# GpSimd's batch loop written out, each batch's row scatter issued behind the next batch's group power

## The chip, the cores and the metric

The kernel runs on one core of one Trainium2 chip. The metric is the device time of one execution in microseconds (us), lower is better. The engines are TensorE (PE; its weight loads are PEld), VectorE (DVE), ScalarE (ACT), GpSimd (POOL) and SyncE (SP, which here only issues DMAs).

## The reference

A transformer block with modulated norms over x of 4 batches, 512 tokens and 256 features. Cut to what matters:

```python
mod = (silu(c) @ wmod).reshape(4, 6, 1, 256)           # sa, ca, ga, sb, cb, gb
h = layernorm(x) * (1 + ca) + sa
# retention with 16 heads of 16 features, decay gamma per head, causal
scores = einsum('bhnd,bhmd->bhnm', q, k) * gamma ** (n - m)
ret = einsum('bhnm,bhmv->bhnv', scores, v)
norm = (ret - mean) * rsqrt(var + 1e-5)                # mean, var per batch and head, over tokens and features
x = x + ga * ((silu(h @ wg + bg) * (norm * gn_w + gn_b)) @ wo + bo)
h = layernorm(x) * (1 + cb) + sb
# 8 experts of 256 -> 512 -> 256, each token goes to its 2 best
logits = h @ gate;  weights = softmax(top2(logits))
x = x + gb * sum over the two experts of weight * (silu(h @ w0) * (h @ w1)) @ wo_e
```

## The kernel before

Retention part. The four batches are done one after another, each in chunks of 128 tokens (4 a batch). For a chunk TensorE makes the scores of four groups of four heads (L1330), VectorE multiplies them by the decay (L912), TensorE multiplies them with the values (L1342) into two PSUM banks `ret`. When chunk 3 of batch b is through, VectorE takes statistics of `ret` (`group_norm`, L917 to L941: L923 and L925, an averaging matmul on TensorE, L935), and the power -1/2 of the variances is GpSimd's: `group_power(b)` waits for L935 and does a tensor_tensor with pow on 128x2 numbers (L452, by the helper of L437). VectorE turns the result into scale and shift (L938 to L941), ScalarE applies them (`group_normed`, L635), VectorE multiplies by the gate (L946), TensorE projects out (`out_rows`, L1366), VectorE adds to x (L957), and SP stores x (L362, 512 KB a batch).

Second norm and routing. VectorE takes row statistics (L781 to L791); `modulate(b)` on GpSimd makes the power of the row variances (L457, by L437), VectorE normalizes the rows into `h2` (`second_norm`, L963 to L968, which waits for that power and for `h2_free`), and GpSimd scales and shifts `h2` (L460, L463). TensorE turns `h2` (L1378) and makes the logits; VectorE picks the two best experts and computes the rows of a DRAM buffer, `routed`, into which each token goes (`idx`, L1030). GpSimd then scatters: `scatter(b)` issues eight indirect DMAs of 128 rows of 266 numbers (L488), and `scatter_done(b)` waits until all have landed and adds to `h2_free`. There is one `h2`, so the next batch's `second_norm` can't write before that.

Order of the work. It is written out by hand for each engine, in program order, with semaphores between the engines. The batches are overlapped: while batch b finishes (group norm, projection out, second norm, routing), the projections and chunks 0 to 2 of batch b+1 are done. GpSimd also makes, for every chunk, a copy of q spread over heads, `qx` (`expand_q`, L447, 128x1024, needed by TensorE for that chunk's scores; ScalarE makes the other half at L628), the scaled output weights (`scale_wo`, L470) and the bias in x (`add_bias`, L477, L480). Its queue in a round of the loop (L512 to L522) is: group power of b; `expand_q(b+1, 0)`; `modulate(b)`; `expand_q(b+1, 1)`; `scale_wo(b+1)`; `expand_q(b+1, 2)`; `add_bias(b+1)`; `expand_q(b+1, 3)`; `scatter(b)`; `scatter_done(b)`. The loop turns three times, for b of 0, 1, 2; the group power of batch 3 stands behind the loop (L553). ScalarE, VectorE and TensorE have loops of three rounds of their own; theirs begin at chunk 3 of a batch and end behind chunk 2 of the next.

Expert part. The rows in `routed` are worked off in 39 tiles of 128 rows, each of one expert. The first 9 tiles (EARLY) are rows of the first batches and are begun while batch 3 finishes: SP loads a tile's rows (L372), `out_rows(3)`, its second norm and its routing are placed between the steps of these tiles. A tile takes TensorE, ScalarE and VectorE work, a gather of gate rows by GpSimd (`fetch_gb`, L527), and an accumulating indirect DMA into the output (`add_rows`, L545). `added_ok` is a count that VectorE waits for before it reuses a buffer of `meta` or `ey`; GpSimd starts it with 4 (L552). The scatter of batch 3 is issued in pairs between the `add_rows` of tiles 2 to 5 (L565).

Of the kernel before, what the change touches and what calls it, by code (L numbers as in the profile page):

```python
# [30 lines left out]
B, S, D = 4, 512, 256  # L31
# [64 lines left out]
def adaln_block(nc, x, wq, bq, wk, bk, wv, bv, wg, bg, wo, bo, gn_w, gn_b, gamma,  # L96
                gate_k, w0, w1, wo_e, c, wmod, out):
    ctx = ExitStack()
    with ctx:  # L99
# [124 lines left out]
        def sems(names):  # L224
            return [sem(n) for n in names.split()]
# [24 lines left out]
        added, added_ok, pool_passed, dve_passed, act_passed = sems("added added_ok pool_passed dve_passed act_passed")  # L250
# [55 lines left out]
        def wait(eng, pair):  # L306
            eng.wait_ge(pair[0], pair[1])

        def settle(eng, pairs, passed):


            for s, v in pairs:
                eng.wait_ge(s, v)
            eng.sem_inc(passed, 1)
# [4 lines left out]
        def grp(b, n):  # L319

            return b * (4 * NC) + n
# [83 lines left out]
        def _(pool):  # L405
# [29 lines left out]
            def power(out_, in_, n, done):  # L435

                g.tensor_tensor(out_, in_, mhalf[:, 0:n], ALU.pow).then_inc(done, 1)  # L437

            def expand_q(b, c):


                if c == 0:
                    wait(pool, front.drains(b, "q0"))
                pool.wait_ge(scored, grp(b, 4 + 4 * (c - 1) + 2))
                q = qT[:, 0, c * P:(c + 1) * P].unsqueeze(1).broadcast_to([P, HPT, P])
                m = hmask[:, :].unsqueeze(2).broadcast_to([P, HPT, P])
                g.tensor_tensor(qx[:, 0, :].rearrange("p (h n) -> p h n", h=HPT), q, m, ALU.mult).then_inc(qx_pool, 1)  # L447

            def group_power(b):

                wait(pool, tail.drains(b, "gn"))
                power(grs[:, :], gve[:, :], FT, grstd)  # L452

            def modulate(b):

                pool.wait_ge(var2, b + 1)
                power(rs2[:, :], ve2[:, :], NC, rstd2)  # L457
                hv = h2[:, :, 0:D]
                pool.wait_ge(h2n_ready, NC * b + NC)
                g.tensor_tensor(hv, hv, gsc[:, bass.ds(b, 1), 2 * D:3 * D].broadcast_to([P, NC, D]),  # L460
                                ALU.mult).then_inc(h2m_ready, 1)
                pool.wait_ge(h2m_ready, b + 1)
                g.tensor_tensor(hv, hv, gsc[:, bass.ds(b, 1), D:2 * D].broadcast_to([P, NC, D]),  # L463
                                ALU.add).then_inc(h2_ready, 1)

            def scale_wo(b):

                if not (isinstance(b, int) and b == 0):
                    settle(pool, [(tail.full, tail.filled(b - 1, "wo23"))], pool_passed)
                g.tensor_tensor(wob[:, :, :], wo_s[:, :, :], gsc[:, bass.ds(b, 1), 0:D].broadcast_to([P, FT, D]),  # L470
                                ALU.mult).then_inc(wob_ready, 1)

            def add_bias(b):

                bog = gsc[:, bass.ds(b, 1), 0:D]
                settle(pool, [(wob_ready, b + 1)], pool_passed)
                g.tensor_tensor(bog, bog, bo_bc[:, :].unsqueeze(1), ALU.mult).then_inc(bog_ready, 1)  # L477
                xb = xs[:, bass.ds(NC * b, NC), :]
                settle(pool, [(bog_ready, b + 1)], pool_passed)
                g.tensor_tensor(xb, xb, bog.broadcast_to([P, NC, D]), ALU.add).then_inc(x1_ready, 1)  # L480

            def scatter(b, tiles):

                if 0 in tiles:
                    settle(pool, [(idx_ready, b + 1), (row_ready, b + 1)], pool_passed)
                for t in tiles:
                    for k in range(TOPK):
                        g.indirect_dma_start(routed, bass.IndirectOffsetOnAxis(ap=idx[:, k, t:t + 1], axis=0),  # L488
                                             h2[:, t, :], None).then_inc(scattered, 16)

            def scatter_done(b):
                pool.wait_ge(scattered, 16 * (TOPK * NC) * b + 16 * (TOPK * NC))
                pool.sem_inc(h2_free, 1)
# [15 lines left out]
            power(rs1[:, 2 * NC:B * NC], ve1[:, 2 * NC:B * NC], 2 * NC, rstd1)  # L509
            expand_q(0, 3)  # L510
            add_bias(0)
            with pool.Fori(0, B - 1) as b:  # L512
                group_power(b)
                expand_q(b + 1, 0)
                modulate(b)
                expand_q(b + 1, 1)
                scale_wo(b + 1)
                expand_q(b + 1, 2)
                add_bias(b + 1)
                expand_q(b + 1, 3)  # L520
                scatter(b, range(NC))
                scatter_done(b)  # L522

# [25 lines left out]
                    weights_lo(i + 3, s + 3)  # L549


            pool.sem_inc(added_ok, 4)  # L552
            group_power(B - 1)  # L553
            pool.wait_ge(gb_out, 16)
            pool.wait_ge(x2_out, 16 * (B - 1))
            fetch_gb(0, 0)
# [1046 lines left out]
```

## Time and profile before

| | us |
|---|---|
| median of 3 runs | 480.45 |
| the three runs | 483.38, 480.45, 478.79 |
| span of the profiled execution, first to last instruction | 489.4 |
| TensorE busy | 426.4 |
| VectorE busy | 298.3 |
| GpSimd busy | 285.5 |
| ScalarE busy | 184.3 |

The profile page gives a span but no time of its own for what lies around the span in the profiled execution. The span alone is 8.9 us longer than the median run, so the profiled execution was slower than the others, and times read from it are compared with each other first and with the median second. The core's mean granted TensorE clock was 0.96 of full speed.

### The profile page before, as it was taken

The numbers are of one execution on the slowest core, as the hardware profiler recorded it, in microseconds if no ns is written. First come the engines' busy times: TensorE is split into PE (matmuls) and PEld (weight loads), VectorE is DVE, ScalarE is ACT, GpSimd is POOL, SyncE is SP. The second block draws the span as 40 slices with busy tenths as digits, with TensorE's granted clock in tenths as the row PEclk, the third lists the DMA queues.
The fourth block names the chain that finished last, engine by engine and source line by source line (L and its number), as shares of the span: only waits on it lengthen the run. The fifth ranks groups of instructions, "written<-read, shape, count | busy, mean of one in ns | idle before, by whom it ended". The sixth has DMA issues, their size and how long they took to land. (4 is left out here: it accounts for less than half of the span.)

```text
span 489.4 us, 8770 instructions
## 1 busy us (share of the span) xinstructions
PE 426.4 (87%) x2160; PEld 284.8 (58%) x2161; DVE 298.3 (61%) x770; ACT 184.3 (38%) x346; POOL 285.5 (58%) x210
## 2 busy tenths in 40 slices
PE   2989999986999949995799868999999999999980
PEld 2345547553565426562366544877777777777760
DVE  4398657582577535784563733776777667766730
ACT  3252453251352415330111103445555455545520
POOL 3003621835256430656116575899989999999971
PEclk9998999998999979999699999999999999999995
DMA  7669951002010101002122564334344433444331
GB/s 244 187 218 376 373 197 45 1 2 89 0 43 0 56 33 43 0 0 89 44 67 51 115 158 86 64 71 75 65 73 79 75 66 65 82 72 74 55 55 21
DMA packets 32892, 42.91 MB, mean 88 GB/s; under 512 B 5244, under 2 KB 26116, under 8 KB 32744
## 3 DMA queue, kind: packets, MB, share of 16 engines
q1 hardware_dynamic: 21784, 27.81, 17.7%
q0 software_dynamic: 9024, 14.59, 16.4%
q10 hardware_dynamic: 2064, 0.28, 0.4%
q8 instruction: 9, 0.15, 0.1%
q14 instruction: 11, 0.09, 0.0%
HBM read 29.85 MB, written 12.81 MB: 87 GB/s over the span
## 5 line engine op out<-in xcount | busy, mean ns | idle before, releaser
L533 POOL TENSOR_TENSOR w_lo<-we,w_hi 128x1024 fp32r<-128x1024 f32 x30 | 88.1, 2938 | 3.2 <-ACT w_hi L706 3.2
L1500 PE MATMUL ps<-we,qx 128*128 x312 | 77.4, 391 | 7.8 <-issue 3.9
L545 POOL DMA_INDIRECT out_dram<-wg_s,meta x39 | 62.3, 1598 | 24.4 <-issue 11.1
L1500 PEld LDWEIGHTS ps<-we,qx 128*128 128x128 f32 x312 | 56.8, 190 | 30.3 <-issue 24.0
L691 ACT COPY qx<-ps 128x512 f32<-128x512 f32 x39 | 22.9, 587 | 121.0 <-PE ps L1492 106.3
L1330 PE MATMUL ps<-qx,kT 128*128 128x512 f32 x128 | 62.0, 606 | 4.5 <-DVE sm L912 4.1
L628 ACT ACTIVATE qx<-qT,hmask 128x128 f32<-128x128 f32 x128 | 39.2, 390 | 42.8 <-PE ps L1330 37.8
L912 DVE TENSOR_TENSOR sm<-ps,dmask 128x512 f32<-128x512 f32 x64 | 43.3, 688 | 12.1 <-PE ps L1330 10.9
L447 POOL TENSOR_TENSOR qx<-qT,hmask 128x1024 f32<-128x1024 f32 x16 | 30.4, 1897 | 29.9 <-ACT qT L609 15.2
L488 POOL DMA_INDIRECT routed<-h,idx x32 | 31.4, 981 | 25.9 <-issue 13.8
L437 POOL TENSOR_TENSOR rs<-ve,mhalf 128x4 f32<-128x4 f32 (+1 forms) x7 | 7.8, 1108 | 62.4 <-DVE ve L791 62.4
L527 POOL DMA_INDIRECT wv_s<-gb_dram,meta x39 | 39.3, 1009 | 7.5 <-issue 7.4
L1170 DVE TENSOR_TENSOR w_halves<-we,w_halves 128x1024 fp32r<-128x1024 f32 x30 | 36.8, 1226 | 10.3 <-ACT w_halves L706 10.3
L1330 PEld LDWEIGHTS ps<-qx,kT 128*128 128x128 f32 x128 | 21.3, 189 | 32.2 <-DVE sm L912 19.8
L1163 DVE SCALAR_TENSOR_TENSOR wg_s<-ps,meta,wv_s 128x256 f32<-128x256 f32 x39 | 18.9, 484 | 30.7 <-DMA wv_s<-gb_dram,meta 20.5
L1471 PE MATMUL ps<-we,xn 128*128 x72 | 36.5, 633 | 0.5 <-issue 0.5
L706 ACT CAST w_hi<-we 128x1024 fp32r x30 | 31.6, 1054 | 0.0
L706 ACT CAST w_halves<-we 128x1024 fp32r x30 | 31.4, 1047 | 0.3 <-issue 0.3
L1149 DVE SCALAR_TENSOR_TENSOR sm<-sm,ps 128x512 f32<-128x512 f32 x39 | 26.8, 687 | 6.0 <-ACT sm L696 5.0
L1480 PE MATMUL ps<-w_halves,rT_halves 128*128 128x512 f32 x60 | 29.3, 489 | 0.0
L1141 DVE CAST rT_halves<-ps 128x256 fp32r<-128x256 f32 x30 | 12.7, 425 | 23.6 <-PE ps L1466 23.6
L1156 DVE TENSOR_TENSOR dmask<-sm,ps 128x512 f32<-128x512 f32 x39 | 26.6, 682 | 0.4
(211 smaller groups left out, 788.8 us busy)
## 6 DMA issues: line engine op xcount, KB each, us to landing
we<-in_ffn_w_kernel_dram SPq DMA_DIRECT2D x16, 512.0 KB, 10.5
we<-in_ffn_wo_kernel_dram SPq DMA_DIRECT2D x8, 512.0 KB, 10.5
wq_s<-routed SPq DMA_DIRECT2D x20, 133.0 KB
wk_s<-routed SPq DMA_DIRECT2D x19, 133.0 KB
xs<-in_attn_x_dram SPq DMA_DIRECT2D x4, 512.0 KB, 13.6
out_dram<-xs SPq DMA_DIRECT2D x4, 512.0 KB, 3.1
we<-in_wmod_dram SPq DMA_DIRECT2D x1, 1536.0 KB, 7.4
gsc<-gsc_dram SPq DMA_DIRECT2D x1, 1536.0 KB, 6.7
```

Of the source, the lines that this page charges most:

```text
L447: g.tensor_tensor(qx[:, 0, :].rearrange("p (h n) -> p h n", h=HPT), q, m, ALU.mult).then_inc(qx_pool, 1)
L488: g.indirect_dma_start(routed, bass.IndirectOffsetOnAxis(ap=idx[:, k, t:t + 1], axis=0), h2[:, t, :], None).then_inc(scattered, 16)
L527: g.indirect_dma_start(gbr[s % 2], None, gb_dram, bass.IndirectOffsetOnAxis(ap=meta[s % 4][:, BAT - D:BAT - D + 1].bitcast(I32), axis=0)). ...
L533: g.tensor_tensor(w_lo[1], expert_up(e, 1), w_hi[1].bitcast(F32), ALU.subtract)\
L545: g.indirect_dma_start(out, bass.IndirectOffsetOnAxis(ap=meta[s % 4][:, TOK - D:TOK - D + 1].bitcast(I32), axis=0), ey[s % 2], None, compu ...
L628: a.activation(qx[:, 1, h * P:(h + 1) * P], qT[:, 1, c * P:(c + 1) * P], ACT.Copy, scale=hmask[:, h:h + 1]).then_inc(qx_act, 1)
L706: a.copy(w_hi[which], expert_up(e, which)).then_inc(w_hi_ready[which], 1)
L912: v.tensor_tensor(sm[:, g, :], sc[n % 2][:, :], dmask[:, 4 * g:4 * g + 4, :].rearrange("p h n -> p (h n)"), ALU.mult).then_inc(masked, 1)
L1170: v.tensor_tensor(w_lo[0], expert_up(e, 0), w_hi[0].bitcast(F32), ALU.subtract)\
L1330: mm(sc[n % 2][:, :], kT[:, ft, cs], qx[:, ft, (g % 2) * 512:(g % 2 + 1) * 512], start=True, stop=True).then_inc(scored, 1)
L1471: last = mm(up_ps[s % 2][which][:, :], rT[s % 2][:, k, :], weights(e, (which * FT + k) * F, F), start=k == 0, stop=k == FT - 1)
L1500: last = mm(down_ps, eit[s % 2][:, k, :], weights(e, 2 * FT * F + k * D, D), start=k == 0, stop=k == KF - 1)
```

## The change

GpSimd's loop over the batches is written out three times, so its semaphore values and addresses are constants. In each of the three copies `group_power(b + 1)` is put ahead of `scatter(b)`; `group_power(0)` stands ahead of them all, and the one of batch 3, which stood behind the loop, is now in the third copy. `pool.sem_inc(added_ok, 4)` is done before the batches instead of behind them. Nothing else is touched, on any engine.

```diff
             add_bias(0)
-            with pool.Fori(0, B - 1) as b:
-                group_power(b)
+            pool.sem_inc(added_ok, 4)
+            group_power(0)
+            for b in range(B - 1):
                 expand_q(b + 1, 0)
                 modulate(b)
                 expand_q(b + 1, 1)
                 scale_wo(b + 1)
                 expand_q(b + 1, 2)
                 add_bias(b + 1)
                 expand_q(b + 1, 3)
+                group_power(b + 1)
                 scatter(b, range(NC))
                 scatter_done(b)
...
-            pool.sem_inc(added_ok, 4)
-            group_power(B - 1)
             pool.wait_ge(gb_out, 16)
             pool.wait_ge(x2_out, 16 * (B - 1))
             fetch_gb(0, 0)
```

## Rows read from the trace of the kernel before

**Rows 1.** The page's first part: engines' busy time.
```profile
PE 426.4 (87%) x2160; PEld 284.8 (58%) x2161; DVE 298.3 (61%) x770; ACT 184.3 (38%) x346; POOL 285.5 (58%) x210
```
**Rows 2.** Waits over the span: total us, times, longest.
```profile
POOL grs L437 <- DVE gve L935: 24.2, 4, 8.5
DVE gst L923 <- remote: 18.1, 3, 8.2
```
**Rows 3.** Timeline of batch 0's end: start us, us, engine line op.
```profile
59.73 1.53 DVE L912 TENSOR_TENSOR sm<-ps,dmask 128x512 f32<-128x512 f32 x2 [2.27 <-PE ps L1330]
...
64.67 1.29 DVE L923 BATCH_NORM_STATS2 gst<-ps 128x6 f32<-128x512 f32 x2 [1.39 <-PE ps L1342]
...
68.23 0.71 POOL L437 TENSOR_TENSOR grs<-gve,mhalf 128x2 f32<-128x2 f32 x1 [8.54 <-DVE gve L935]
...
71.26 1.44 ACT L635 ACTIVATE sm<-ps,gB,gA 128x512 f32<-128x512 f32 x2
...
78.60 0.41 SPq L362 DMA_DIRECT2D out_dram<-xs  x1
...
80.74 1.01 POOL L437 TENSOR_TENSOR rs<-ve,mhalf 128x4 f32<-128x4 f32 x1 [9.93 <-DVE ve L791]
...
82.63 1.28 DVE L867 SCALAR_TENSOR_TENSOR z<-sm,z 128x512 f32<-128x512 f32 x2
83.84 1.38 DVE L967 TENSOR_SCALAR h<-xs,mv,rs 128x256 f32 x4
```
**Rows 4.** Timeline of batch 1's end.
```profile
108.55 1.29 DVE L912 TENSOR_TENSOR sm<-ps,dmask 128x512 f32<-128x512 f32 x2 [0.66 <-DVE carry L1031]
...
117.97 0.96 POOL L488 DMA_INDIRECT routed<-h,idx  x1 [0.30 <-issue]
...
122.54 0.72 POOL L437 TENSOR_TENSOR grs<-gve,mhalf 128x2 f32<-128x2 f32 x1 [3.60 <-DVE gve L935]
```
**Rows 5.** Timeline of batch 2's end.
```profile
163.83 1.29 DVE L912 TENSOR_TENSOR sm<-ps,dmask 128x512 f32<-128x512 f32 x2 [0.61 <-PE ps L1330]
164.02 1.06 POOL L488 DMA_INDIRECT routed<-h,idx  x1 [4.90 <-DVE idx L1030]
...
172.99 0.96 POOL L488 DMA_INDIRECT routed<-h,idx  x1 [0.31 <-issue]
...
180.42 0.72 POOL L437 TENSOR_TENSOR grs<-gve,mhalf 128x2 f32<-128x2 f32 x1 [6.47 <-DVE gve L935]
181.13 1.89 POOL L447 TENSOR_TENSOR qx<-qT,hmask 128x1024 f32<-128x1024 f32 x1
181.18 1.86 DVE L938 SCALAR_TENSOR_TENSOR gA<-grs,gnw_s 128x2 f32<-128x2 f32 x1 [0.84 <-POOL grs L437]
```
**Rows 6.** Stretches: us, busy PE, PEld, DVE, ACT, POOL (instructions), clock, DMA share, GB/s.
```profile
168.50:175.50 7.00, 1.98 (x4) 0.68 (x4) 0.00 (x0) 0.08 (x1) 4.24 (x5) 1.00 0.27 99
...
174.00:175.00 1.00, 0.00 (x0) 0.00 (x0) 0.00 (x0) 0.00 (x0) 0.00 (x0) 1.00 0.37 136
...
175.50:182.50 7.00, 5.08 (x9) 2.70 (x10) 3.51 (x9) 1.10 (x2) 2.08 (x2) 0.52 0.00 0
```
**Rows 7.** Timeline of batch 3's end.
```profile
230.95 0.96 POOL L488 DMA_INDIRECT routed<-h,idx  x1 [0.30 <-issue]
...
229.13 0.16 DVE L1128 TENSOR_SCALAR tabi<-ps 1x9 int32<-1x9 f32 x1 [2.04 <-remote]
...
233.65 1.30 DVE L923 BATCH_NORM_STATS2 gst<-ps 128x6 f32<-128x512 f32 x2 [4.30 <-remote]
...
237.51 0.72 POOL L437 TENSOR_TENSOR grs<-gve,mhalf 128x2 f32<-128x2 f32 x1 [5.59 <-DVE gve L935]
...
238.27 0.16 DVE L938 SCALAR_TENSOR_TENSOR gA<-grs,gnw_s 128x2 f32<-128x2 f32 x1 [0.84 <-POOL grs L437]
...
253.28 1.03 POOL L437 TENSOR_TENSOR rs<-ve,mhalf 128x4 f32<-128x4 f32 x1 [9.61 <-DVE ve L791]
```
**Rows 8.** DMA issues of the page: KB each, us to landing.
```profile
out_dram<-xs SPq DMA_DIRECT2D x4, 512.0 KB, 3.1
```

## The prediction

> **What bounds the kernel now.** I read the page's first part, then the waits, then the timeline of each batch's end, then stretches of it. No engine fills the span: TensorE is busy for 87% [rows 1], so the time is set by chains between engines, in the retention part by the one that runs once a batch from the last chunk through the group norm to the projection out. In the waits the reader is to see that GpSimd's group power waited four times for VectorE's variances, 24.2 us together, and never for its own scatter, and that VectorE's first statistics (L923) waited three times, 18.1 us, for something that the profile only calls "remote" [rows 2].
>
> The timeline shows where. In batch 0, with no scatter about, the decay product of chunk 3 starts at 59.73, the statistics at 64.67 and the group power at 68.23, so the power is 8.50 behind the product's start [rows 3]. In batch 1 it is 122.54 - 108.55 = 13.99 behind it [rows 4], in batch 2 180.42 - 163.83 = 16.59 [rows 5]. The surplus over batch 0 is 5.5 and 8.1 us. In batch 3 the statistics sat idle for 4.30, behind a table entry that had itself waited 2.04, both for "remote" [rows 7]; I put its surplus at 4.3 to 6.3, say 5.5. In all three a scatter is in flight. From 168.5 to 175.5 VectorE did nothing at all, TensorE 1.98 us, ScalarE 0.08 us, while GpSimd issued and the DMA engines moved data [rows 6]; the last scatter left GpSimd at 172.99 + 0.96 = 173.95 [rows 5], and traffic was still seen after 174.0 [rows 6]. So three engines stand still until the scatter has landed, for a reason that the profile doesn't name.
>
> The profiled execution isn't the ordinary one: its span is 489.4 and the median run 480.45. At least 8.9 us of this standing still may be absent from the runs that count. What then remains of it? The real wait lies under it: the group power stands in GpSimd's queue behind `scatter` and `scatter_done`. In batch 2 the eight issues take 173.95 - 164.02 = 9.93 [rows 5]; to this come the landing of the last (between 1.0 and 1.6 by rows 5 and 6; I take 1.5) and the turn of the loop (estimate 0.4, between 0 and the 0.9 that rows 5 leave between it and the next event). Without the stall the power could start 8.50 behind the product, at 172.3; the queue lets it start at 173.95 + 1.9 = 175.9. It is late by 3.6 and the profile can't show it because the variances were held up longer still.
>
> **The change, part by part.** *Group power ahead of the scatter, removed wait.* Batch 1: ready at 108.55 + 8.50 = 117.05, queue free at 117.97 + 0.96 + 1.9 = 120.8 [rows 4], gain 3.8. Batch 2: gain 3.6. Batch 3: the statistics could begin between 229.35 - 2.04 = 227.3 and 229.35 (233.65 less its idle 4.30), the power 3.86 behind (237.51 - 233.65), at 231.2 to 233.2; the queue is free at 230.95 + 0.96 + 1.9 = 233.8 [rows 7], late by 0.6 to 2.6. There TensorE also has expert tiles to do, so I count 1.0. Everything behind the power in these batches (scale and shift, L635 at 3.03 behind it in batch 0 [rows 3], the gate product, the projection out) hangs on it directly. Sum of gains 3.8 + 3.6 + 1.0 = 8.4. Ends: 0 in each, if the variances really come as late as the profile says, and the whole surplus, 19.1, if the standing still goes as well.
>
> *Loop written out.* It takes away one turn and some register arithmetic on GpSimd per round; in the trace that is hidden, since GpSimd then waits 3.60 and 6.47 for the variances [rows 4, 5]. Counted above in the 0.4, otherwise nothing. More instructions must be read once; no row prices that, I bound it by 0 and the 0.9 above, three times, and take 0, as GpSimd waits in each round. Moving `added_ok` costs nothing: nobody reads it before the tiles of the expert part.
>
> *The scatter behind the power, added delay.* What stood right behind the power now stands behind eight issues and their landing. Let T be the power's start. It ends at T + 0.7, the first DMA can go at T + 1.1 (the settling waits ahead of it, estimate 0.4, a little over the 0.30 between two issues [rows 4]), the eighth is out at T + 11.0, landed at T + 12.5. `expand_q(b+1, 0)`, which ran from T + 0.7 [rows 5], runs from T + 12.5 to T + 14.4, and `modulate`'s power from T + 14.4 to T + 15.4. In batch 0 that power ran at T + 12.5 (80.74 - 68.23), as soon as its data was there, but VectorE, which uses it, came to its instruction only at T + 15.6 (83.84), behind the gates (L867) [rows 3]. So 1.9 us of delay are hidden by VectorE's own queue with 0.2 to spare; TensorE's scores of chunk 0, which need `qx`, come later still. `h2_free` at T + 12.5 is in time for the same instruction. The cover is gone if the scatter lands later. It may: SP stores x at T + 10.4 (78.60), 512 KB that take 3.1 us to land [rows 3, 8], across the last two scatters, which only traffic of the scatters' own queue surrounded before. At the bad end the landing slips by 3.1 and costs 2.9; and `expand_q` now runs next to the gates (L867, 1.28), which at worst stand still for the overlap, 1.3. Against that, VectorE's L938 took 1.86 beside `expand_q` in batch 2 and 0.16 in batch 3 where none ran beside it [rows 5, 7]; the 1.7 us are hidden, since ScalarE takes its own queue first. I take 0.9 a batch, nearer to the row with cover, for batches 1 and 2: 1.8, with ends 0 and 8.4.
>
> Behind the power of batch 3 stand the scatter of batch 2 and then the first gather for the experts and `modulate(3)`. The scatter ends at T + 12.5, `modulate`'s power ran at T + 15.8 (253.28 - 237.51) [rows 7]: covered by 3.3. Cost 0.
>
> Two rules of the Trainium skill bear on this. The page "SBUF — State Buffer", section "SBUF: two separate sides", says that VectorE and GpSimd share one pair of ports under an exclusive lock and that an instruction of VectorE with two inputs in SBUF blocks against one of GpSimd that reads SBUF. The trace agrees (1.86 against 0.16). By it the new place of `expand_q`, beside L867, is the price and not the gain. "DMA: Bandwidth & Descriptors", section "Queues, rings and completion order", says that a DMA engine goes round between its queues packet by packet; by it the last two scatters would share with the store of x and the 2.9 above would be paid at least in part, the sum becoming 8.4 - 5.8 = 2.6. No row here shows the two together.
>
> *Sum.* -8.4 + 1.8 = -6.6 on the profiled 489.4, that is 482.8. What lies around the span and how much of the stall the ordinary runs have is unknown; the terms are durations and waits of single places, so I take the same 6.6 off the median: 480.45 - 6.6 = 473.9.
>
> **The rivals.** *A: the stall stays where it is.* In each of the three stalls VectorE, ScalarE or TensorE also turns its own loop over, so the cause may be theirs and not the scatter's; rows 2 speak for it (the power never waited for the scatter). Against it: in batch 3 nobody turns back, and it stalls too. Then the gain is 0, the variances come late, and the delayed `modulate` costs 0 to 1.8: 480.5 to 482.3, say 481.0.
>
> *B, the other side: the stall goes with the scatter and hits harder.* The standing still began some 4.5 us behind the first scatter in batch 2 (164.02 to 168.5) and lasted until the last had landed. Moved, it would lie from T + 5.6 to T + 12.5, over the projection out, VectorE's sum into x and the row statistics, all one chain. Three new stalls of at most 6.9 make 20.7 against the 19.1 removed, and `modulate` late on top, 0 to 4.4 a batch, say 1.9, gives 20.7 + 3.8 - 19.1 = +5.4: 485.9. It decides from the point where more than 6.4 of each 6.9 is exposed. Against it: TensorE has projections with data at hand there, so I expect less of it exposed.
>
> *C: the stall vanishes altogether.* TensorE's clock was at half (0.52) for 7 us behind the stall of batch 2 [rows 6]; without idle time that goes too. Gain up to 19.1 less 1.8 less what the ordinary runs don't have, 8.9, and plus the clock, some 2 (TensorE was busy for 5.08 us at half clock in rows 6, which is 2.5 saved): 480.45 - 10.4 = 470.1. I hold it apart from the forecast only by the size.
>
> *D: the store collides.* Gain 8.4, price 5.8 or more: 477.9.
>
> **How the numbers follow.** Forecast (gain of 4.9 to 9) 0.38, C 0.16, D 0.18, A 0.18, B 0.10. A measurement of this kernel tells about 1%, 4.8 us, from no change, so faster means under 475.6: nearly all of the forecast and of C and a little of D, together 0.56; slower over 485.3: most of B, 0.08; the rest, 0.36, is within 1%. The range from 468 to 482 takes in all but the far end of C and B and leaves out some 0.2.
>
> **What would show it.** In the profile after, in batches 1 and 2, the group power starts 8.5 to 9.5 behind chunk 3's first decay product and the "remote" waits of L923 are gone. The first scatter stands about 1.1 behind the group power, the eighth about 11.0, `expand_q` at about T + 12.5; L938 takes 0.16 there; L967 starts within T + 15.6 to T + 17.5. TensorE's clock stays at 1.00 behind chunk 3. The forecast is wrong if L923 still waits as long (A), if a new wait for "remote" of several us shows between T + 5 and T + 13 on VectorE or ScalarE (B), or if L967 waits for GpSimd's power by over 2 us (D).

## The result and the profile after

| | before | after |
|---|---|---|
| median, us | 479.75 (4 runs, 478.79 to 483.38) | 472.53 (4 runs, 472.16 to 473.98) |
| ratio | | 0.986, 95% interval 0.982 to 0.990 |
| profiled execution, us | not given | 472.42 |
| its span, us | 489.4 | 470.7 |

The change takes 7.2 us, 1.4%. In the profiled execution after, the time is 1.7 us above the span. The profiled execution of before must then have taken some 491, and the four runs beside it 480: they are not executions of one kind, and the experiments show a difference between chips that fits.

The page after, first part; then waits over the span (total us, times, longest):

```profile
PE 423.6 (90%) x2160; PEld 283.9 (60%) x2161; DVE 298.5 (63%) x770; ACT 184.3 (39%) x346; POOL 285.1 (61%) x210
```
```profile
POOL grs L437 <- DVE gve L935: 49.7, 4, 14.6
```

No engine's instructions have changed in number, and the busy times stay within 3 us [rows 1]. GpSimd now waits 49.7 us for the variances of the group norm instead of 24.2 [rows 2], because it stands ready for them with nothing ahead. The row with "remote" of [rows 2] has no counterpart: no wait of any engine is put down to "remote" after the change.

Timeline after, the end of batch 1, which answers to [rows 4], with the rows that answer to the end of [rows 3]:

```profile
108.47 1.29 DVE L912 TENSOR_TENSOR sm<-ps,dmask 128x512 f32<-128x512 f32 x2 [0.66 <-DVE carry L1031]
...
113.35 1.30 DVE L923 BATCH_NORM_STATS2 gst<-ps 128x6 f32<-128x512 f32 x2 [1.33 <-PE ps L1342]
...
116.92 0.71 POOL L437 TENSOR_TENSOR grs<-gve,mhalf 128x2 f32<-128x2 f32 x1 [13.38 <-DVE gve L935]
...
117.66 0.16 DVE L938 SCALAR_TENSOR_TENSOR gA<-grs,gnw_s 128x2 f32<-128x2 f32 x1 [0.82 <-POOL grs L437]
...
117.86 1.22 POOL L488 DMA_INDIRECT routed<-h,idx  x1 [0.24 <-issue]
...
119.94 1.44 ACT L635 ACTIVATE sm<-ps,gB,gA 128x512 f32<-128x512 f32 x2
...
124.64 0.69 DVE L957 TENSOR_TENSOR xs<-xs,ps 128x512 f32 x1 [1.33 <-PE ps L1366]
...
127.05 0.96 POOL L488 DMA_INDIRECT routed<-h,idx  x1 [0.31 <-issue]
...
127.27 0.40 SPq L362 DMA_DIRECT2D out_dram<-xs  x1
...
131.12 1.90 POOL L447 TENSOR_TENSOR qx<-qT,hmask 128x1024 f32<-128x1024 f32 x1 [3.11 <-DMA routed<-h,idx]
...
131.31 2.85 DVE L867 SCALAR_TENSOR_TENSOR z<-sm,z 128x512 f32<-128x512 f32 x2
...
132.97 1.49 POOL L437 TENSOR_TENSOR rs<-ve,mhalf 128x4 f32<-128x4 f32 x1
...
134.50 1.39 DVE L967 TENSOR_SCALAR h<-xs,mv,rs 128x256 f32 x4 [0.34 <-POOL rs L437]
```

The group power stands 116.92 - 108.47 = 8.45 behind the first decay product, where batch 0 had 8.50 and batch 1 of before 13.99. The eight DMAs follow it, and `expand_q` waits for their landing (the bracket names the DMA). VectorE's L967, which in batch 0 found its data ready [rows 3], now waits for GpSimd's power. Batches 2 and 3 after:

```profile
167.21 0.71 POOL L437 TENSOR_TENSOR grs<-gve,mhalf 128x2 f32<-128x2 f32 x1 [13.14 <-DVE gve L935]
...
218.86 0.71 POOL L437 TENSOR_TENSOR grs<-gve,mhalf 128x2 f32<-128x2 f32 x1 [14.64 <-DVE gve L935]
```

Stretches after, 7 us from chunk 3's last values on (busy PE, PEld, DVE, ACT, POOL, clock, DMA share, GB/s):

```profile
113.40:120.40 7.00, 7.00 (x19) 3.24 (x20) 2.66 (x11) 2.42 (x4) 2.90 (x3) 1.00 0.05 19
163.70:170.70 7.00, 7.00 (x19) 3.24 (x20) 2.62 (x11) 2.42 (x4) 2.73 (x3) 1.00 0.05 19
```

TensorE is busy throughout at full clock. The second line answers to [rows 6], which had 1.98 us of work in 7.00 and then half clock.

### The profile page after: what moved, and what is told of

It is laid out like the page before. It is cut to its first block and busy times, and to the rows that moved or that the text cites. A ratio compares the mean times of both kernels' runs of the same rounds, so it can differ in the third digit from the quotient of the medians.

```text
span 470.7 us, 8724 instructions
## 1 busy us (share of the span) xinstructions
PE 423.6 (90%) x2160; PEld 283.9 (60%) x2161; DVE 298.5 (63%) x770; ACT 184.3 (39%) x346; POOL 285.1 (61%) x210
## 5 line engine op out<-in xcount | busy, mean ns | idle before, releaser
L535 POOL TENSOR_TENSOR w_lo<-we,w_hi 128x1024 fp32r<-128x1024 f32 x30 | 85.8, 2862 | 3.3 <-ACT w_hi L706 3.3
L691 ACT COPY qx<-ps 128x512 f32<-128x512 f32 x39 | 22.9, 587 | 120.6 <-PE ps L1492 120.6
L1471 PE MATMUL ps<-we,xn 128*128 x72 | 38.6, 663 | 0.5 <-issue 0.5
L437 POOL TENSOR_TENSOR grs<-gve,mhalf 128x2 f32<-128x2 f32 x4 | 2.8, 707 | 49.7 <-DVE gve L935 49.7
```

The lines of the kernel that those rows point to most:

```text
L535: g.tensor_tensor(w_lo[1], expert_up(e, 1), w_hi[1].bitcast(F32), ALU.subtract)\
L1471: last = mm(up_ps[s % 2][which][:, :], rT[s % 2][:, k, :], weights(e, (which * FT + k) * F, F), start=k == 0, stop=k == FT - 1)
```

## The experiments

Two theories stood at the start. F, the queue wait: the group power waits behind the issues and the landing of the scatter, 3.6 us in batches 1 and 2 and about 1 in batch 3. A: the standing still for "remote" is the kernel's own. The experiments ran on three chips, numbered 12, 14 and 15, and every ratio is to runs of before on the same chip. The record doesn't say on which chip the result and the first profile of before were taken.

**Before once more, and its two parts alone** (chip 12).

> The kernel before, unchanged, to see its profile a second time. Theory F (the queue wait): the standing still of three engines belonged to that one profiled execution, the ordinary one has the group power late behind the landing of the scatter. Then the time is 479 to 481, the span within 3 us of it, L923 has no wait for 'remote' over 1 us in batches 1 and 2, and the group power stands 12.2 +- 0.6 behind chunk 3's first decay product in batches 1 and 2 (8.5 in batch 0), released by the scatter's landing. Rival A (the stall is the kernel's own): the profile again shows 5 to 8 us of 'remote' waits on L923, a span of 487 to 491 and the power 14 to 17 behind the product.

Measured: 494.44, before beside it 493.53; ratio 1.001, interval 0.998 to 1.005. Waits and timeline of its batch 1:

```profile
DVE gst L923 <- remote: 19.1, 3, 6.6
```
```profile
108.28 1.29 DVE L912 TENSOR_TENSOR sm<-ps,dmask 128x512 f32<-128x512 f32 x2 [0.66 <-DVE carry L1031]
...
117.71 0.96 POOL L488 DMA_INDIRECT routed<-h,idx  x1 [0.30 <-issue]
118.00 1.30 DVE L923 BATCH_NORM_STATS2 gst<-ps 128x6 f32<-128x512 f32 x2 [6.17 <-remote]
...
122.34 0.72 POOL L437 TENSOR_TENSOR grs<-gve,mhalf 128x2 f32<-128x2 f32 x1 [3.66 <-DVE gve L935]
```

Theory F as I had put it falls here: the standing still isn't peculiar to one profiled execution. On this chip none of the 33 executions of this kernel took less than 489.9, the profiled one 490.3 among them. These lines also correct the reading that the engines stand still until the scatter has landed: here VectorE starts again at 118.00, before the eighth issue is out at 118.67, and in the first profile of before it did so too (L923 at 117.71, the eighth issue out at 118.93 by [rows 4]). In batches 2 and 3 of these two profiles it starts between 0.1 and 1.7 us behind the end of the last issue.

```diff
-            with pool.Fori(0, B - 1) as b:
+            for b in range(B - 1):
                 group_power(b)
```

> GpSimd's loop written out, the order as before. Theory F: the wait stays, only the turn of the loop ahead of the power goes (0.4 us, twice or three times): ratio to before 0.997 to 1.001, 479 +- 1. Rival 'the writing out did it': 0.986, as the whole change (472.5).

Measured: 492.02, ratio 0.997, interval 0.994 to 1.000. Its L923 waits as long as in before:

```profile
DVE gst L923 <- remote: 19.1, 3, 6.8
```

Writing the loop out brings 1.5 us, by the interval between 0.2 and 2.9. It can't be said from this run alone what it brings without the standing still, because here GpSimd waits 4.80 us for the variances behind the turn of the loop, which hides the turn. The Trainium skill ("Runtime: NRT & Kernel Launch", section "Instruction fetch mechanics") gives a branch that needs a fetch as a reason to unroll; no run here shows whether a fetch is in these 1.5 us.

```diff
+            pool.sem_inc(added_ok, 4)
+            group_power(0)
             with pool.Fori(0, B - 1) as b:
-                group_power(b)
...
                 expand_q(b + 1, 3)
+                group_power(b + 1)
                 scatter(b, range(NC))
                 scatter_done(b)
...
-            pool.sem_inc(added_ok, 4)
-            group_power(B - 1)
```

> The loop kept, with the new order in it (group power of batch b+1 ahead of the scatter, the one of batch 0 ahead of the loop, added_ok moved as in the change). Theory F: nearly the whole gain, ratio 0.985 to 0.989 (472.5 to 474.5), the power 8.5 behind the product in batches 1 and 2. Rival 'the writing out did it': ratio 0.998 to 1.002.

Measured: 475.81, ratio 0.967, interval 0.962 to 0.971. Timeline of its batch 1:

```profile
110.27 1.29 DVE L912 TENSOR_TENSOR sm<-ps,dmask 128x512 f32<-128x512 f32 x2 [0.66 <-DVE carry L1031]
...
115.15 1.29 DVE L923 BATCH_NORM_STATS2 gst<-ps 128x6 f32<-128x512 f32 x2 [1.33 <-PE ps L1342]
...
118.71 0.71 POOL L437 TENSOR_TENSOR grs<-gve,mhalf 128x2 f32<-128x2 f32 x1 [13.37 <-DVE gve L935]
...
133.44 2.11 POOL L447 TENSOR_TENSOR qx<-qT,hmask 128x1024 f32<-128x1024 f32 x1 [3.62 <-DMA routed<-h,idx]
```

On this chip the order alone carries the gain, and it is 17.7 us, over twice what I expected: with the scatter away from the end of chunk 3 L923 waits for nothing but TensorE's values, and the standing still goes there too. The last line prices the turn of the loop: `expand_q` waits 3.62 behind the eighth issue, where the next kernel, with the loop written out and on the same chip, has 3.09, so a turn is 0.5 us. The standing still doesn't go everywhere. The waits of this kernel still have, in the expert part,

```profile
ACT qx L691 <- remote: 9.7, 1, 9.7
DVE xn L1139 <- remote: 4.2, 1, 4.2
```

where GpSimd issues the scatters of batch 3 between the tiles' own indirect DMAs. The profile of before has both too (9.9 and 4.5), and in its batches 1 and 2 ScalarE stood still beside VectorE (L609, up to 7.1 us, "remote"); the profile after has none of these.

```diff
-                group_power(b + 1)
+                if b + 1 < B - 1:
+                    group_power(b + 1)
                 scatter(b, range(NC))
                 scatter_done(b)
+                if b + 1 == B - 1:
+                    group_power(b + 1)
```

> The changed kernel, with the group power of batch 3 put back behind the scatter of batch 2 and its landing. Theory F with my term of 1.0 us: 473.5, ratio 0.987 to 0.990. If batch 3's term was sized too small because the whole lateness of 0.6 to 2.6 us counts: 474 to 475.2. If the expert tiles hide it all: 472.5. In the profile the power of batch 3 is 1 to 3 us later, and what follows tells whether the routing of batch 3 moves with it.

Measured: 478.92, ratio 0.970, interval 0.966 to 0.974. Its batch 3 (the kernel has three lines more, L926 is L923):

```profile
221.28 1.29 DVE L926 BATCH_NORM_STATS2 gst<-ps 128x6 f32<-128x512 f32 x2 [5.64 <-remote]
...
225.13 0.72 POOL L437 TENSOR_TENSOR grs<-gve,mhalf 128x2 f32<-128x2 f32 x1 [5.47 <-DVE gve L938]
```

In batches 1 and 2 the wait is gone, in batch 3, where the scatter again comes first, it is back with 5.6 us. So at the end of a batch the standing still comes, on this chip, with the scatter lying across it. It costs 3.1 us against the kernel with the order alone (478.92 - 475.81). The intervals of the two ratios overlap a little, and this kernel has its loop written out and the other hasn't, so the cost of the order in batch 3 is rather larger than 3.1; this is a size, not a proof.

**The change on another chip, and two ways to split the difference** (chip 14).

> The changed kernel once more, on the chip on which its variants run now. On the chip of the first experiments the kernel before took 493.5 and the reordered loop 475.8, so the ratio there was 0.967, not 0.986. Theory S (the standing still is real, lasts as long as a scatter is in flight across the end of chunk 3, and its size differs between chips): ratio 0.964 to 0.972 on such a chip, 0.984 to 0.988 on one like that of the result; no 'remote' wait on L923 in either. Theory F alone (only the queue wait of 3.6, 3.6 and 1.0) would give 0.984 to 0.988 everywhere.

Measured: 473.58, before beside it 480.38; ratio 0.985, interval 0.983 to 0.987, the result over again. So there are chips on which before takes 480 and one on which it takes 494. No reordered kernel ran on both kinds: the one with the order alone took 475.81 on chip 12, the change 473.58 here.

```diff
-                group_power(b + 1)
                 scatter(b, range(NC))
+                group_power(b + 1)
                 scatter_done(b)
```

> The changed kernel with the group power put between the eighth issue and scatter_done. Theory F: only the landing (1.5 to 1.9) is taken off the old wait, the power 10.2 to 10.8 behind the decay product instead of 8.5. Theory S: the scatter is in flight across chunk 3's end again, L923 waits 5 to 6 us for 'remote', the power is 14 to 15.5 behind the product and the time within 2 us of the kernel before.

Measured: 471.71, ratio 0.983, interval 0.979 to 0.987. Timeline of its batch 1, and the last three lines of batch 3:

```profile
109.12 1.29 DVE L912 TENSOR_TENSOR sm<-ps,dmask 128x512 f32<-128x512 f32 x2 [0.66 <-DVE carry L1031]
...
114.00 1.29 DVE L923 BATCH_NORM_STATS2 gst<-ps 128x6 f32<-128x512 f32 x2 [1.33 <-PE ps L1342]
...
118.54 0.96 POOL L488 DMA_INDIRECT routed<-h,idx  x1 [0.30 <-issue]
...
119.53 0.74 POOL L437 TENSOR_TENSOR grs<-gve,mhalf 128x2 f32<-128x2 f32 x1
...
120.30 0.16 DVE L938 SCALAR_TENSOR_TENSOR gA<-grs,gnw_s 128x2 f32<-128x2 f32 x1 [2.81 <-POOL grs L437]
...
121.23 1.90 POOL L447 TENSOR_TENSOR qx<-qT,hmask 128x1024 f32<-128x1024 f32 x1 [0.97 <-DMA routed<-h,idx]
...
134.44 1.38 DVE L967 TENSOR_SCALAR h<-xs,mv,rs 128x256 f32 x4
...
208.52 0.69 DVE L912 TENSOR_TENSOR sm<-ps,dmask 128x512 f32<-128x512 f32 x1
...
217.55 0.96 POOL L488 DMA_INDIRECT routed<-h,idx  x1 [0.30 <-issue]
218.59 0.72 POOL L437 TENSOR_TENSOR grs<-gve,mhalf 128x2 f32<-128x2 f32 x1
```

Here the queue wait is seen bare: eight DMAs lie across the end of chunk 3 and L923 doesn't wait for "remote"; the power starts 0.03 behind the eighth issue, 10.41 behind the product, and L938 waits 2.81 for it instead of 0.82. The landing ends at 121.23, 1.73 behind that issue. In before the power stood behind this too, so at +12.1 or later. The kernel is as fast as the whole change, or a little faster, so the change pays for the early power elsewhere. And it is 8.7 us faster than before, though the power only moved ahead of the landing and the turn of the loop. By the 1.7 here and the 0.5 above that is 2.2 us in each of three batches, at most 6.6; the rest can't be placed, as no profile of before was taken on a chip of this kind.

```diff
-                group_power(b + 1)
-                scatter(b, range(NC))
+                scatter(b, range(NC - 1))
+                group_power(b + 1)
+                scatter(b, (NC - 1,))
                 scatter_done(b)
```

> The changed kernel with the scatter split: six of the eight DMAs ahead of the group power (7.6 us of issue, which fit before the variances), two behind. Theory F: the power stays at +8.5, the landing and so expand_q and modulate come 7 us earlier, 1.9 us a batch saved at L967: 2 to 4 us faster than the changed kernel. Theory S: six DMAs are in flight until 9 to 9.5 us behind the product, so L923 is held until then (+9.3 instead of +4.9), the power comes at +13, and the kernel is 6 to 12 us slower than the changed one.

Measured: 468.39, ratio 0.975, interval 0.973 to 0.977: 12.0 us below before and 5.2 below the change. Timeline of its batch 1 (one line more above VectorE's code, L968 is L967):

```profile
115.03 0.96 POOL L488 DMA_INDIRECT routed<-h,idx  x1 [0.30 <-issue]
...
116.60 0.72 POOL L437 TENSOR_TENSOR grs<-gve,mhalf 128x2 f32<-128x2 f32 x1 [0.61 <-DVE gve L936]
...
117.52 1.03 POOL L488 DMA_INDIRECT routed<-h,idx  x1 [0.20 <-issue]
...
129.11 1.04 POOL L437 TENSOR_TENSOR rs<-ve,mhalf 128x4 f32<-128x4 f32 x1 [4.96 <-DVE ve L792]
...
130.99 1.28 DVE L868 SCALAR_TENSOR_TENSOR z<-sm,z 128x512 f32<-128x512 f32 x2
...
132.19 1.38 DVE L968 TENSOR_SCALAR h<-xs,mv,rs 128x256 f32 x4
...
215.47 0.72 POOL L437 TENSOR_TENSOR grs<-gve,mhalf 128x2 f32<-128x2 f32 x1 [2.85 <-DVE gve L936]
```

Six issues end 0.6 us before the variances are there, so the power isn't late, and everything behind it is as in batch 0: the second power at T + 12.5, L968 at T + 15.6 without a wait (T is the start of the group power). The gain over the change is larger than the 2 to 4 expected. From batch 1's power to batch 3's this kernel takes 215.47 - 116.60 = 98.87, the change 218.86 - 116.92 = 101.94: 3.1 of the 5.2 us lie there, the rest isn't placed. The standing still that theory S expected of six DMAs doesn't come on this chip.

> The same with four DMAs ahead of the power (5.0 us) and four behind. Theory S with 'until landed': the four have landed at about +6.7, L923 comes at +6.7 instead of +4.9 and the power at +10.3: some 2 us a batch slower than the changed kernel in the power, 1.9 us a batch gained at L967, so about equal. If the standing still needs more than 4 us of issue in a row: no delay of L923, the time 2 to 4 us below the changed kernel. Theory F: the same 2 to 4 below.

The edit is the same with two tiles on either side. Measured: 469.83, ratio 0.978, interval 0.975 to 0.980; the difference to six ahead isn't clear of noise. Both versions beat the change and before on this chip.

**Before a third time, and the store of x** (chip 12 again).

> The kernel before a third time, to see its profile where the time of before is 480 (two chips so far: 493.5 with the standing still in every profile, 480.4 without it in any variant). If this chip gives about 480: theory F has no 'remote' wait on L923, the group power of batches 1 and 2 at +12.0 to +12.4 behind the decay product, with GpSimd waiting for the scatter's landing, not for L935; batch 3 at +12 to +13. If it gives about 490 or more: the standing still again, as in the profile on which the prediction rests.

Measured: 494.83 beside 494.36. This is again the chip with the standing still, so there is no profile of before at 480:

```profile
DVE gst L923 <- remote: 20.1, 3, 8.2
```

```diff
                 wait(sp, tail.drains(b, "wo23"))
+                if done_sem is x2_out:
+                    sp.wait_ge(h2_free, b + 1)
                 sp.dma_start(out_v...
...
-            with sp.Fori(0, B - 1) as b:
+            for b in range(B - 1):
                 store_x(b, x2_out)
```

> The changed kernel, SP's store of x held until the scatter of the batch before has landed (and SP's loop written out). Rival D (the store of x holds the last two scatters up): the eighth DMA lands 1.5 to 1.7 us behind its issue instead of 3.0, expand_q starts at T + 12.7 instead of T + 14.1, L967 at T + 15.6 to T + 16.2 instead of 17.5: 2 to 3.5 us faster than the changed kernel. If the late landing is the scatter's own: T + 14.1 stays, and the time too.

Measured: 471.00 beside before at 494.36; ratio 0.951, interval 0.946 to 0.957. Timeline of its batch 1 (two lines more, the names of the lines are shifted by 2):

```profile
127.05 0.96 POOL L490 DMA_INDIRECT routed<-h,idx  x1 [0.30 <-issue]
...
129.87 0.39 SPq L364 DMA_DIRECT2D out_dram<-xs  x1
...
130.00 1.90 POOL L449 TENSOR_TENSOR qx<-qT,hmask 128x1024 f32<-128x1024 f32 x1 [1.99 <-DMA routed<-h,idx]
...
131.32 1.73 DVE L869 SCALAR_TENSOR_TENSOR z<-sm,z 128x512 f32<-128x512 f32 x2
...
133.38 1.38 DVE L969 TENSOR_SCALAR h<-xs,mv,rs 128x256 f32 x4 [0.34 <-POOL rs L439]
```

With the store held back `expand_q` waits 1.99 for the landing instead of 3.11 after the change, and L969 stands at 133.38 instead of 134.50, with the group power at 116.92 in both. So rival D's mechanism, the store that delays the landing, is real with 1.1 us a batch, a third of the 3.1 of its worst case. Two other things differ between the two profiles, the chip and SP's loop; but a kernel on this same chip 12 with the store where the change has it waits 3.09. The kernel is 4.8 us below the order-only one of the same chip, but the two didn't run side by side and differ in both loops, so I take only the 1.1 from this run.

**Two repeats** (chip 15).

> The split scatter (six DMAs ahead of the group power) a second time, in the hope of a chip on which the kernel before takes some 494. There, theory S1 (the standing still needs a scatter in flight across the end of chunk 3 and ends when it has landed): L923 at +9 to +9.5 behind the decay product instead of +4.9, 'remote' waits of 4 us three times, the time near 480 or above. Theory S2 (it needs more than six DMAs in a row): L923 at +4.9, about 468 to 470, as on the other chip. On a chip with before at 480: 468.4 +- 1 again.

> All eight DMAs ahead of the group power, but not their landing, a second time. On a chip with before at 494: the standing still as in before (L923 at +9 to +12), 488 to 494. On a chip with before at 480: 471.7 +- 1.5 again.

Measured, before beside them 479.95: 469.50, ratio 0.977, interval 0.974 to 0.980, and 472.20, ratio 0.985, interval 0.981 to 0.988. Both within 1.1 us of their times on chip 14, without "remote" waits. Whether the split scatter causes the standing still on a chip like 12 (S1 or S2) stays open; it was never run there.

## Why the prediction was right

- *Sum.* Forecast 473.9 with -6.6 from the median; measured 472.53 and -7.2. The path was the forecast one: power ahead, scatter behind, a part given back at `modulate`. But the two sides of the sum are both larger than I had them, and that the number came within 1.4 us is in part luck, as the two errors cancel.
- *The queue wait under the standing still, 3.8 and 3.6.* Right. With no stall and eight DMAs ahead the power stands at +10.41, the landing ends 1.70 behind it, and the turn of the loop is 0.5 more, which makes 12.6 against 8.45: 4.2 (I had 1.9 for landing and turn, the runs show 2.2). This is put together from runs of other kernels, since before has no profile without the standing still. Not all of it was gain: with the power 1.96 late, VectorE's second norm came at T + 14.9 instead of T + 15.6 (134.44 - 119.53), so 0.7 of a lateness is made up by work done meanwhile. Gain about 3.5 a batch, an estimate.
- *Batch 3, 1.0.* Too low, by more than a factor of two. With the power behind the eighth issue that issue ends at 217.55 + 0.96 = 218.51, 9.99 behind the product (208.52); with landing and turn the power would stand at +12.2, where the change has 218.86 - 209.03 = 9.83: late by 2.4, inside the 0.6 to 2.6 that I gave, not by 1.0. The sum of these estimates is 3.5 + 3.5 + 2.4 less the price of 3.1 measured over two batches, which makes 6.3 of the measured 6.8 to 7.2. The run that puts batch 3 back, 3.1 slower than the one with the order alone, is from the chip with the stall and bears on this only loosely.
- *The delayed `modulate`, 0.9 a batch.* Too low, by nearly a factor of two. L967 comes at T + 17.6 (134.50 - 116.92) instead of 15.6, just outside the band that I gave. Two terms make it: the store of x makes the landing 3.1 us (131.12 - 128.01) instead of the 1.5 that I took, of which the held store gives 1.1 back; and GpSimd's power takes 1.49 instead of 1.01. `expand_q` beside the gates also stretches L867, from 1.28 a pair [rows 3] to 2.85, but L867 ends before the power does and L967 still waits 0.34 for it, so this costs nothing more. From batch 1's power to batch 2's it is 167.21 - 116.92 = 50.29, where the split version has 48.5: 1.8 for this batch, and 3.1 for two. Both rules of the Trainium skill that I had cited spoke for a price, the lock on the shared ports ("SBUF — State Buffer", section "SBUF: two separate sides") and the round between queues ("DMA: Bandwidth & Descriptors", section "Queues, rings and completion order"). The runs agree with both in direction (L867's 2.85 beside `expand_q`, the landing's 3.1 beside the store), and I should have moved the value toward them.
- *Loop written out, 0 beyond the 0.4 for the turn.* Nearly right. The run has 1.5 us, with 0.2 to 2.9 as its interval, and the traces 0.5 for a turn. On the chips without the standing still the turn lies open, so some 1.5 of the 7.2 us may be the writing out and not the order; the order alone wasn't run there. The 0.9 that I gave as the turn's upper end isn't in rows 5.
- *`added_ok`, "nobody reads it before the tiles of the expert part".* True but beside the point. VectorE takes up the first tile's `meta` between L931 and L935 of batch 3 and waits there for `added_ok`. Left behind the loop, the count would wait for the power, the power for L935 and L935 for the count. The move is a condition of the new order; this is read from the code.
- *What the standing still was.* Here the reasoning was wrong, though the number held. I put at least 8.9 us of it down to the profiled execution alone. It goes with the chip: on chip 12 it is in both profiles of before (19.1 and 20.1 us on L923), and no execution of before there took less than 489.9, on chips 14 and 15 no profile shows it, even with eight DMAs ahead of the power. Nor does it last until the scatter has landed, as I read it: in batch 1 it ends before the eighth issue does. Rival C, that it vanishes, is what happens at the batches' ends on chip 12, with -17.7 for the order alone; in the expert part it stays (L691, 9.7). The profile shown of before must be from a chip of that kind and the runs beside it from the other; that is an inference from 489.4 against 480.45.
- *B* doesn't happen: with the scatter from T + 0.9 to T + 11.1 on, VectorE's first sum into x stands at T + 7.72 (124.64 - 116.92), as in batch 0 (T + 7.73), and on chip 12 the order-only kernel has it there too. *A* falls by the order-only run on chip 12. *D* is real and is about a third of its worst case. In *B* my point of balance was off: with the 3.8 for `modulate` in its sum it is (19.1 - 3.8) / 3 = 5.1 of each 6.9, not 6.4.

## What to carry to other kernels

A small operation that others wait for shouldn't stand in a queue behind a block of DMA issues and their completion; but before the whole block goes behind it, count how many issues fit into the time in which the operation waits for its data anyway. Here six of eight fitted, and the split was worth 5 us more than the move on a chip without the standing still, the only kind on which it ran. A wait that hides another one (the variances late, so that the queue's own wait isn't seen) has to be worked out from an undisturbed round of the same kernel, and if the span of the profile is longer than the timed runs, ask which chip each came from.

## What the runs showed of the hardware

On one of three chips, chip 12, VectorE waited up to 8.2 us and ScalarE up to 7.1 at the ends of batches for something that the profile can't name, while GpSimd issued eight indirect DMAs of 128 rows in a row across the end of a chunk, though TensorE's work ahead of them was recorded as done (in batch 2 of the first profile of before, whose chip isn't recorded, the values were done at 168.48 and VectorE read them at 175.60). The same eight DMAs 9 us later, across the projections, held nobody up there. In the profiles of the other two chips, eight DMAs across the end of the chunk show nothing of it. What is shown: it depends on the chip and on where the scatter stands; the kernel before takes 14 us more on that chip than on the others. For the reordered kernels the difference between chips isn't measured. What the standing still is remains open, and so does whether fewer DMAs in a row avoid it.

Four smaller sizes: a turn of GpSimd's loop is 0.5 us. The eighth of eight indirect DMAs landed 1.7 us behind the end of its issue by itself, 3.1 with a store of 512 KB beside it, 2.0 with the store held back. Two scalar_tensor_tensors of VectorE on 128x512 took 2.85 us beside a tensor_tensor of GpSimd and 1.28 without. A pow of GpSimd on 128x4 took 1.49 us beside them and 1.01 without.
